# First-layer rows that carry their mean and variance, and an attention mix moved to VectorE, in a fused MoE + attention + MoE kernel

## The reference, cut to what matters

```
x = x + 0.5 * ffn(layernorm(x))       # top-1 routing, 32 experts, capacity 640 rows
x = x + attn(layernorm(x))
x = x + 0.5 * ffn(layernorm(x))       # the same expert weights

ffn:   out = xt + gate * (silu(xe @ Wg) * (xe @ Wu)) @ Wd        (rows over capacity keep only xt)
attn:  delta = softplus((x @ Wp.T) @ Wdelta.T + b)
       dA = exp(delta * A1) * B1;      dB = cumsum(delta * B1, over the sequence)
       y  = dA * sum(x * Cs) + dB * sum(Cs) + residual
```

## Time and profile before

| what | us |
|---|---|
| median of 3 runs (lowest, highest) | 1657.67 (1656.46, 1665.96) |
| the profiled execution, its own time | 1659.85 |
| span of the profile | 1658.0 |

### The profile page before, as it was taken

How to read it: one execution, slowest core, us unless ns; L and a number is a source line. 1 busy time by engine, 2 the same in 40 slices (tenths; PEclk the granted TensorE clock), 3 DMA queues, 4 the chain that set the end, 5 groups by cost and what they waited for, 6 DMA issues and landing times. The chain is left out here.

```text
span 1658.0 us, 32704 instructions
## 1 busy us (share of the span) xinstructions
PE 1384.7 (84%) x10686; PEld 1297.6 (78%) x10686; DVE 1190.8 (72%) x3211; ACT 1167.4 (70%) x2458; POOL 776.3 (47%) x989
## 2 busy tenths in 40 slices
PE   4345531799999999779999999998747999999997
PEld 3223320699999999779999999998636999999997
DVE  5366644577788787567799888889655777777875
ACT  7568851577777777468888888887545777777774
POOL 0046566143443434334447778777452434434343
PEclk8555555799999999989999999999867999999999
DMA  9977844566666766340222223311115444444541
GB/s 366 372 235 250 267 151 144 176 207 226 219 220 204 237 220 196 144 143 14 78 78 82 88 79 93 94 56 48 38 43 151 123 123 135 138 140 123 157 139 36
DMA packets 196888, 250.10 MB, mean 151 GB/s; under 512 B 24650, under 2 KB 182008, under 8 KB 192624
## 3 DMA queue, kind: packets, MB, share of 16 engines
q1 hardware_dynamic: 169072, 204.23, 38.3%
q0 software_dynamic: 27648, 43.78, 7.5%
HBM read 128.05 MB, written 152.17 MB: 169 GB/s over the span
## 5 line engine op out<-in xcount | busy, mean ns | idle before, releaser
L978 PE MATMUL ps<-xs,ws 128*128 128x320 f32 x3072 | 466.3, 311 | 3.7 <-DVE hf L932 3.7
L978 PEld LDWEIGHTS ps<-xs,ws 128*128 128x128 f32 x3072 | 456.0, 190 | 4.8 <-issue 4.8
L347 POOL DMA_INDIRECT slots<-xn,r x256 | 261.6, 1022 | 239.1 <-issue 167.9
L805 POOL DMA_INDIRECT x_rows<-ys,oidx x160 | 155.9, 975 | 251.9 <-DVE ys L917 174.2
L805 POOL DMA_INDIRECT out<-ys,oidx x160 | 156.0, 975 | 248.7 <-DVE ys L917 170.7
L978 PE MATMUL ps<-ws,hs 128*128 128x256 f32 x1920 | 261.9, 288 | 11.0 <-DVE ys L917 7.5
L978 PEld LDWEIGHTS ps<-ws,hs 128*128 128x128 f32 x1920 | 238.7, 190 | 24.4 <-issue 22.3
L932 DVE TENSOR_TENSOR hf<-ps,sg 128x320 f32<-128x320 f32 x256 | 125.8, 492 | 144.5 <-issue 101.8
L415 PE MATMUL ps<-cf,xn 128*128 128x128 f32 x512 | 110.7, 355 | 109.2 <-ACT xn L369 95.4
L826 ACT CAST xs<-ps 128x512 fp32r<-128x512 f32 (+1 forms) x192 | 98.5, 514 | 130.0 <-PE ps L971 130.0
L415 PEld LDWEIGHTS ps<-cf,xn 128*128 128x128 f32 x512 | 73.9, 178 | 144.8 <-ACT xn L369 118.2
(11 more groups left out here) (119 smaller groups left out, 2428.3 us busy)
## 6 DMA issues: line engine op xcount, KB each, us to landing
slots<-zero SPq DMA_DIRECT2D x32, 1300.0 KB, 18.7
xg<-slots SPq DMA_DIRECT2D x62, 650.0 KB
x<-in_x SPq DMA_DIRECT2D x32, 512.0 KB, 10.8
x_rows<-x SPq DMA_DIRECT2D x32, 512.0 KB
wraw<-in_w_gate SPq DMA_DIRECT2D x64, 256.0 KB
wraw<-in_w_up SPq DMA_DIRECT2D x64, 256.0 KB
wraw<-in_w_down SPq DMA_DIRECT2D x64, 256.0 KB
x<-x_rows SPq DMA_DIRECT2D x32, 512.0 KB, 4.8
```

The lines of the kernel that those rows point to most:

```text
L347: nc.gpsimd.indirect_dma_start(out=self.slots, out_offset=bass.IndirectOffsetOnAxis(ap=self.slot[:, t % self.xr, k:k + 1], axis=0), in_=se ...
L805: nc.gpsimd.indirect_dma_start(out=rows, out_offset=bass.IndirectOffsetOnAxis(ap=OIDX[:, e % YR, k:k + 1], axis=0), in_=YS[:, e % YR, k, : ...
L978: ins = pe.matmul(dst, left(a, k), right(b, k), start=(n == 0), stop=(n == len(terms) - 1))
```

## The change

Three things are changed together.

1. The rows of the first layer's result get two more columns, mean and variance (HX = 258). In route, `dve_factors` makes them for the base rows with three more small operations per group of tiles. In `experts(0)`, DVE makes them for the finished rows with `moments` (a bn_stats and a bn_aggr per tile) and POOL's scatter waits for them. In exchange the low halves of the weights are made by POOL there (`split_w` on POOL, one after each of the scatters of tiles 1, 2 and 3, for the expert after the next).
2. Attention drops `a_stats` and `a_aggr`; `a_rstd` reads mean and variance from the loaded rows, in two pieces per batch instead of four, and waits for the DMA itself.
3. In attention the mix moves from PE to DVE: ACT's `d_a` gets the log of |u| into its bias (`size_bias`, once per batch), so that it makes |u|*exp; DVE adds sign(u)*c*cumsum in place (`mix`, two scalar_tensor_tensor of 128x256 per pair, right after `scan`), and PE multiplies by one diagonal of signs instead of two diagonals: two matmuls per tile instead of four.

```diff
+HX = H + 2
...
-        x1_rows = nc.dram_tensor("x1_rows", [T, H], F32, kind="Internal").ap()
+        x1_rows = nc.dram_tensor("x1_rows", [T, HX], F32, kind="Internal").ap()
...
-                dve.tensor_scalar(self.s1[:, r, k], self.rb[:, r, k], 0.5, 1.0, ALU.mult, ALU.add)
+                ins = dve.tensor_scalar(self.s1[:, r, k], self.rb[:, r, k], 0.5, 1.0, ALU.mult, ALU.add)
+                if not self.own:
+
+                    ins.then_inc(self.widened.sem, 1)
+                    mean, var = (self.stream.moment(CH * lo, n, w) for w in range(2))
+                    dve.tensor_scalar(mean, self.mn[:, r, k], -1.0, None, ALU.mult)
+                    dve.wait_ge(self.widened.sem, self.widened.at(2 * g + 1))
+                    dve.tensor_tensor(var, self.s1[:, r, k], self.s1[:, r, k], ALU.mult).then_inc(self.widened.sem, 1)
+                    dve.wait_ge(self.widened.sem, self.widened.at(2 * g + 2))
+                    dve.scalar_tensor_tensor(var, self.ve[:, r, k], -EPS, var, ALU.add, ALU.mult)
...
+                            if turn == 1:
+                                pool.wait_ge(ysum.sem, ysum.at(NQ * e + q + 1))
                             apart(pool)
                             for k in range(2 * q, 2 * q + widths[q] // P):
+                                if turn == 0:
+                                    pool.wait_ge(row_done.sem, row_done.at(ET * e + k + 1))
+                                    apart(pool)
 
                                 if k >= 2 and e + 1 < end:
                                     pool.wait_ge(gu.sem, gu.at(4 * e + 4 + k - 1))
                                     out=rows, out_offset=bass.IndirectOffsetOnAxis(ap=OIDX[:, e % YR, k:k + 1], axis=0),
                                     in_=YS[:, e % YR, k, :], in_offset=None, bounds_check=T - 1, oob_is_err=False,
                                 ).then_inc(y_out[e % YR], 16)
-
+                                if turn == 0 and e + 2 < end and k >= 1 and k < 4:
+                                    split_w(e + 2, k - 1)
...
+                    def split_w(e, k):
+                        pool.wait_ge(whi.sem, whi.at(3 * e + k + 1))
+                        w = slice(2 * k, 2 * k + 2)
+                        apart(pool)
+                        nc.gpsimd.tensor_tensor(WS[:, e % 2, 1, w], WRAW[:, w], WS[:, e % 2, 0, w].bitcast(F32),
+                                                ALU.subtract).then_inc(wlo.sem, 1)
+
+                    if turn == 0:
+                        for e in (first, first + 1):
+                            for k in range(3):
+                                split_w(e, k)
...
+                    def moments(e, lo, hi):
+                        dve.wait_ge(ysum.sem, ysum.at(NQ * e + (hi - 1) // 2 + 1))
+                        for k in range(lo, hi):
+                            dve.bn_stats(BSE[:, e % 2, k, :], YS[:, e % YR, k, 0:H]).then_inc(row_bn.sem, 1)
+                        for k in range(lo, hi):
+                            dve.wait_ge(row_bn.sem, row_bn.at(ET * e + k + 1))
+                            dve.bn_aggr(YS[:, e % YR, k, H:HX], BSE[:, e % 2, k, :]).then_inc(row_done.sem, 1)
...
-                            if m < 3 and more:
+                            if m < 3 and more and turn == 1:
                                 split_w(e + 1, m)
                             if m == 3:
                                 out_index(e)
+                            if turn == 0 and e > first and m < 2:
+                                moments(e - 1, 3 + m, 4 + m)
...
+                        if turn == 0:
+                            moments(e, 0, 3 if more else ET)
...
+                roots = [(lo, hi, -9) for lo, hi in ((0, 4), (4, TB))]
+                roots += [(TB * a + lo, TB * a + lo + TB // 2, NC * a + at) for a in range(1, BATCH)
+                          for lo, at in ((0, -9), (TB // 2, -6))]
...
+                    def a_rstd(g):
+                        lo, hi, step = roots[g]
+                        a, r = lo // TB, lo // TB % 2
+                        if a >= 2:
                             pool.wait_ge(normed.sem, normed.at(NC * (a - 1)))
-                        pool.wait_ge(stats.sem, stats.at(p + 1))
+                        for q in range(lo // 4, hi // 4):
+                            stream.arrived(pool, q)
...
-                        nc.gpsimd.tensor_tensor(RA[:, r, k], VEA[:, r, k], NHALF[:, 0:4],
+                        nc.gpsimd.tensor_tensor(RA[:, r, k], VEA[:, r, k], NHALF[:, 0:1].to_broadcast([P, n]),
...
+                    def size_bias(a):
+                        act.wait_ge(sized.sem, sized.at(a + 1))
+                        apart(act)
+                        act.activation(LB[:, a % 2, 0, :], UV[:, a % 2, 4, :], ACT.Ln).then_inc(size_links.sem, 1)
+                        act.wait_ge(size_links.sem, size_links.next())
+                        for h in range(HC):
+                            ins = act.activation(LB[:, a % 2, 1, h:h + 1], LB[:, a % 2, 0, h:h + 1], ACT.Identity,
+                                                 bias=ABD[:, h:h + 1])
+                        ins.then_inc(biased.sem, 1)
+
                     def d_a(n):
+                        a = n // NC
+                        if n % NC == 0:
+                            act.wait_ge(biased.sem, biased.at(a + 1))
                         act.wait_ge(softplus_done.sem, softplus_done.at(n + 1))
                         act.wait_ge(residual_done.sem, residual_done.at(n - 1))
                         for h in range(HC):
                             ins = act.activation(YT[:, n % 2, h, :], AB[:, n % 2, h, :], ACT.Exp,
-                                                 bias=ABD[:, h:h + 1], scale=A1[:, h:h + 1])
+                                                 bias=LB[:, a % 2, 1, h:h + 1], scale=A1[:, h:h + 1])
...
-                        for n in range(2):
-                            for h in range(HC):
-                                ins = dve.tensor_scalar(DIAG[:, a % 2, n, h, :], IDENT, uv[:, n, h:h + 1], None, ALU.mult)
+                        dve.scalar_tensor_tensor(uv[:, 2, :], uv[:, 0, :], -1.0, uv[:, 0, :], ALU.mult, ALU.max)
+                        dve.tensor_scalar(uv[:, 5, :], uv[:, 0, :], 0.0, 2.0, ALU.is_ge, ALU.mult).then_inc(f_links.sem, 1)
+                        dve.wait_ge(f_links.sem, f_links.next())
+                        dve.tensor_scalar(uv[:, 4, :], uv[:, 2, :], TINY, None, ALU.max).then_inc(sized.sem, 1)
+                        dve.tensor_scalar(uv[:, 6, :], uv[:, 5, :], -1.0, None, ALU.add).then_inc(f_links.sem, 1)
+                        dve.wait_ge(f_links.sem, f_links.next())
+                        dve.tensor_tensor(uv[:, 3, :], uv[:, 1, :], uv[:, 6, :], ALU.mult).then_inc(f_links.sem, 1)
+                        for h in range(HC):
+                            ins = dve.tensor_scalar(DIAG[:, a % 2, h, :], IDENT, uv[:, 6, h:h + 1], None, ALU.mult)
                         ins.then_inc(diag.sem, 1)
+                        dve.wait_ge(f_links.sem, f_links.next())
...
-                        dve.wait_ge(residual_done.sem, residual_done.at(n - 1))
+                        if n >= 2:
+                            dve.wait_ge(mixed.sem, mixed.at(n - 1))
...
+                    def mix(n):
+                        dve.wait_ge(scanned.sem, scanned.at(n + 1))
+                        dve.wait_ge(da_done.sem, da_done.at(n + 1))
+                        apart(dve)
+                        for h in range(HC):
+                            ins = dve.scalar_tensor_tensor(YT[:, n % 2, h, :], CC[:, n % 2, h, :],
+                                                           UV[:, n // NC % 2, 3, h:h + 1], YT[:, n % 2, h, :],
+                                                           ALU.mult, ALU.add)
+                        ins.then_inc(mixed.sem, 1)
...
-                        pe.wait_ge(da_done.sem, da_done.at(n + 1))
-                        pe.wait_ge(scanned.sem, scanned.at(n + 1))
+                        pe.wait_ge(mixed.sem, mixed.at(n + 1))
                         pe.wait_ge(x_added.sem, x_added.at(n))
                         for j in range(CH):
                             for i, (a, b, k) in enumerate(terms):
                                 pe.matmul(ps[:, BY, j * H:(j + 1) * H], XS[:, n % 3, a, k, j * P:(j + 1) * P],
                                           WA[:, 4 + 2 * b + k, :], start=(i == 0), stop=False, skip_group_check=True)
-                            for i, src in enumerate((YT, CC)):
-                                for h in range(HC):
-                                    ins = pe.matmul(ps[:, BY, j * H + h * P:j * H + (h + 1) * P],
-                                                    src[:, n % 2, h, j * P:(j + 1) * P], DIAG[:, t % 2, i, h, :],
-                                                    start=False, stop=(i == 1 and h == HC - 1),
-                                                    skip_group_check=True)
```

(4 more changed lines are left out.)

104 lines of the change are left out of this document (49 added, 55 removed).

## The result

The changed kernel is slower: 1784.66 us median (four runs, 1777.17 to 1788.88) against 1657.07 for the kernel before on the same chip; ratio 1.076, 95% interval 1.071 to 1.080. The forecast was 1638, with 1614 to 1673 for 8 in 10.

| stretch | before, us | after, us | difference |
|---|---|---|---|
| start to first expert | 301.7 | 307.9 | +6.2 |
| first to last expert start (31 experts) | 382.1 | 479.7 | +97.6 |
| last expert start to first `x_new` | 56.1 | 63.7 | +7.7 |
| first batch of attention | 55.5 | 50.1 | -5.4 |
| second batch | 58.6 | 55.4 | -3.2 |

A forecast was written before the change was run, and what follows sets the result against it. PE was taken to bound attention and experts(0), with DVE bounding attention after the change. Terms -23 - 6 - 1 + 6 + 1.5 + 2 = -20.5 gave 1639.4, stated as 1638; range 1614 to 1673 for 8 in 10.

The forecast's parts named there:

- Experts(0): +6 forecast: Experts(0): low halves on POOL delay the weights, PE stalls 0.15 to 0.2 us per expert; +6 over thirty experts.
- rival 4: Experts(0) and attention: POOL holds DVE, `h_lo` up to 1.0 us per expert, `mix` 0.5 per pair; 1692, chance 0.04.
- So the row says that POOL gives way: Argument against POOL holding DVE: a POOL operation of 0.55 us stretched to 1.458, a scan never exceeded 0.906.
- rival 1: Experts(0): POOL late with low halves, so weights late for ACT; stall 1.4 us per expert, 1673, chance 0.13.
- Attention, full batches: 55.3 forecast: Steady attention batches: DVE's floor 54.3 plus 1.0 us of waiting gives 55.3, a gain of 3.8 per batch.
- The floor: Full attention batch: least time per engine, PE 52.1 us and DVE 54.3, so DVE would be the bound.
- POOL loses two of four `a_rstd` per batch ... It stays below 47 of 55 us: Attention: power of 8 columns taken as 1.9 us on POOL, whose load stays below 47 of 55 us.
- rival 2: Attention: `mix` waits about 0.8 us in six of eight steps, batches stay 58.5 to 59.5; 1661, chance 0.22.
- First batch: First attention batch: PE 48.5, DVE 47, taken as 49.5 us; -6 (-7 to -3).
- last pairs: Last seven attention pairs and tail: +0.8 for mix, -0.88 for PE; written as -1 (-6 to +6).
- seam: Last expert into attention: last scatter +3.6 us, attention starts without four bn_stats, -2.0; total +1.5 (-2 to +5).
- Route: Route: three small DVE operations per group hidden, wide stores under 1% more bytes; +2 (0 to +8).

The follow-up runs named there:

- e14: Changed kernel with a POOL memset (zeros) in place of each low half in experts(0): ratio 1.015, 12.24 us per expert.
- e12: Changed kernel with each low half on POOL made as two instructions of 256 columns: ratio 1.052, 14.15 us per expert.
- e11: Changed kernel with low halves on DVE, `a_rstd` in four pieces, `d_a` ahead of `act_norm`, mix behind `x_new`: ratio 0.996, full batch 55.7 us.
- e5: Changed kernel with attention's `a_rstd` in four pieces per batch again: ratio 1.067, full batch 58.1 us.
- e9: Changed kernel with low halves on DVE, `a_rstd` in four pieces and `d_a` ahead of `act_norm`: ratio 1.007, full batch 58.4 us.
- e6: Changed kernel with only the wide rows left (low halves on DVE, mix on PE as before): ratio 1.011, full batch 59.1 us.
- e10: e9 without route's three operations per group for mean and variance, rows still wide: ratio 1.008, first expert at 287.3 us.
- e2: Kernel before with only POOL's low halves in experts(0) added: ratio 1.045, 14.64 us per expert.
- e3: Changed kernel with `out_index` moved from block m = 3 to m = 0 of experts(0): ratio 1.082, 15.63 us per expert.
- e16: e11 unchanged, on a chip where the kernel before takes 1658.0 us: ratio 1.039, 14.27 us per expert.
- e7: Kernel before with only the mix moved to DVE: ratio 1.017, full batch 64.0 us.

## Why the prediction was wrong

**Experts(0): +6 forecast, +97.6 measured.** The step that failed is the one in rival 4, "So the row says that POOL gives way". It was drawn from the extremes of two lines: a POOL operation stretched to 1.458 and a scan that never exceeded 0.906. Even these extremes are holds: the seven scans of 0.896 to 0.906 us, against a median of 0.750, all began 0.63 to 0.67 us after the same POOL line had, with less than 0.4 us of it left. And the trace of the kernel before has a line that met POOL earlier in its run and shows DVE held by much more: L489, a tensor_tensor with both inputs in SBUF, once per batch. DVE and POOL, timelines at the same moment:

```profile
1011.85 1.25 DVE L489 TENSOR_TENSOR r<-cf,r 128x512 bf16<-128x512 f32 x1
```

```profile
1011.97 1.58 POOL L337 TENSOR_SCALAR x<-x,r 128x256 f32<-128x256 f32 x2
```

Its median is 0.691. The first of POOL's two operations took 0.58 there, as when alone, the second 1.02. Of the six L489 of this size in attention, the one that met no L337 took 0.69, the other five 0.76 to 1.25. So each engine can be held by the other. I took the extremes of a line that runs often, and did not look at what happened where the two lines overlapped. The Trainium skill ("SBUF — State Buffer", section "Who interferes with whom") had the rule, and a finer one than I used: DVE with two SBUF inputs contends with a POOL instruction that reads SBUF, not with one that only writes; a copy, cast or tensor_scalar in a two-port mode contends too. The trace agrees on what is held (`h_lo` up to 1.64 us under the subtraction, the five-column tensor_scalar 1.88) and so does e14 (0.49 under the memset). It does not bear out that whoever is first holds the other: L489 started 0.12 us ahead of POOL and the tensor_scalar 0.57 us ahead, and both were held. Rival 4 got a chance of 0.04.

The size in rival 4 was off as well: 1.0 per expert, for one held `h_lo`; measured 3.1. Three low halves hold three operations of DVE in a row, each delay goes on through ACT's high half to the next block, and behind a wait of 2.5 us PE's clock falls in half of the experts. Its other half, a hold of up to 0.5 us of `mix` per pair, hardly came: in the full batch `mix` took 0.502 on average against a median of 0.483. The mark named (`h_lo` above 0.6 us) was the right one.

The other numbers of that part held: a low half 1.302 us (1.2 taken), the load requested 11.3 us after block 0 (11.4 marked). ACT did not wait for the weights, because an expert of 15.5 us and not 12.3 gives the load 3 us more; rival 1 was hidden and not wrong, as e12 shows, where ACT waits for them for up to 3.0 us.

**Attention, full batches: 55.3 forecast, 63.2 measured.** The floor was right: with the waits repaired DVE is busy 52.7 and PE 53.7 of 56.7 us (e11), and the batch takes 55.7. `mix` at 0.483 us (median) cost 0.06 more than the row taken for it. The step that failed is "POOL loses two of four `a_rstd` per batch ... It stays below 47 of 55 us". The power was priced well (1.81 for 1.9 taken), and POOL's busy time is 42.2; but the question was what stands behind the 3.9 us on POOL. The text asked who is queued behind `mix` on DVE and not what is queued ahead of `d_a` on ACT: rival 2 (chance 0.22) had the right wait, placed it at 0.8 us in six of eight steps and let a batch stay at 58.5 to 59.5. It is 5.3 us once per batch. The bundle costs 5.1 us of a batch (e5), and the place of the mix 2.7 (e11 against e9).

**First batch, last pairs, seam.** -5.4 for -6 forecast, -0.7 for -1. The last scatter ended 8.8 us after the last `y_sum` (8 marked). From the start of the last expert to the last scatter e6, in which nothing is held, takes 4.1 us more than before (3.6 forecast). In the changed kernel it is 5.2, and another 2.5 lie between the last scatter and the first `x_new`, where 2.0 were to be gained; no run traced these.

**Route.** +6.2 for +2, inside the 0 to 8 given. On this kind of chip that is within the spread of one and the same route (300.3 to 311.1); on the others the wide rows cost 9 us. The three operations are hidden (e10), the stores were priced by their bytes and cost more.

## What to carry to other kernels

Work moved to an idle engine is not free because the engine is idle: ask what it shares with the engine that it relieves, and test it on moments at which the two engines' instructions overlap, with operands like those of the instruction that would be held, not on the largest duration of a line. When a wait is added on one engine, follow the awaited instruction's own queue upstream, engine by engine, until it ends at work that is certainly done; and before joining small pieces into one, see what stands behind the piece. When a repair makes a stage shorter, price again the waits that were hidden before it. A gain of less than 1% that loads an engine to 91% may turn into a loss on another chip of the same type, so compare on more than one.

## What the runs showed of the hardware

- An `h_lo` (both inputs in SBUF) that starts under a POOL subtraction of 128x512 ends 0.35 to 0.36 us after it, whenever it started: all 240 cases in the traces of the changed kernel, e2 and e3.
- A DVE instruction that starts 0.56 to 0.63 us ahead of the subtraction, under a scatter, can be held until the subtraction ends: the five-column tensor_scalar took 1.88 us and not 0.16 (30 cases in the changed kernel), an `h_lo` 2.29 and not 0.49 (8 cases in e3).
- Not held: under the subtraction of 128x512, bn_stats (0.42) and bn_aggr (0.18); under that of 128x256 in e12, a tensor_tensor with one input in PSUM (0.48 to 0.49, 36 cases). A POOL memset of 128x512 (0.554 us) held no `h_lo` (0.49 to 0.50).
- On POOL a subtraction of 128x512 takes 1.302 us and one of 128x256 takes 0.757, a power of four columns 1.04 and of eight 1.81.
- After a PE wait of 2.5 us the next twelve matmuls took either 1.70 us at a granted clock of 1.00 (2.4 GHz) or 2.58 us at 0.59, between the two levels.
- Two chips, one kernel: 12.37 or 14.27 us per expert (e11, e16). The kernel before differs between these kinds of chip in other places, as far as stages that e2 and e7 left as they were can show: route takes 280 and 277 us there against 302, the last seven pairs of attention 50 (e2) against 62, and an expert 12.28 (e7) against 12.33.
